# The weighted values of a key block in two pieces, the second half of the queries one slot later than the first

## The chip, the cores and the metric

One core of a Trainium2 chip runs the whole program. The metric is the time of one execution on the device in microseconds (us), lower is better. The kernel before took 1381.69 us in the median of 3 runs (1381.51 to 1382.86).

## The reference

The input x has 8 images of 256 channels and 32 x 32 pixels. Each image goes through a softmax attention over its 1024 pixels with 8 heads of 32 channels, then a linear attention and a small feed-forward net, each with a residual. The part that the change touches is the first:

```python
xn = _group_norm(xf, gn_w, gn_b)
qkv = jnp.einsum('oc,bcl->bol', w_qkv, xn) + b_qkv[None, :, None]
weight = jnp.einsum('bct,bcs->bts', q * scale, k * scale)
weight = jax.nn.softmax(weight.astype(jnp.float32), axis=1)
a = jnp.einsum('bts,bcs->bct', weight, v)
```

The softmax runs over the queries t (axis 1), so each key s has its own sum, and the values of a key can be divided by it before the last product. Behind it come the output projection and the residual, the layer norms, an elu attention with rotary angles and a short convolution ("lepe"), and a Haar transform with fc1, gelu and fc2.

## The kernel before, in words

The 8 images are pipelined. A body of the program runs the softmax attention of image i, and between its steps the later layers of image i-1 ("post" tiles: proj, x1T, lnT, qk, kT, kv, den, out, uT, ll, fc1, fc2, rT) and the norm and the projections of what comes next (gn, pq, pk, pv). A prologue stands before the first image and an epilogue behind the last. Image 0 is the body "first" (no post tiles, but small "warm" matmuls that keep TensorE busy), images 1 to 6 are "steady", image 7 is "last".

A body has 64 units: 2 groups of 4 heads, 8 blocks of 128 keys per group, 4 heads per block. For unit s, TensorE writes the scores of 128 keys and 1024 queries into one of two PSUM tiles, ps_s[s % 2], with two matmuls of 512 columns (`scores`, L636). VectorE takes the negated maximum over the queries (L1025), and ScalarE writes the exponentials to probs and their sum to sums (L887). probs holds two blocks. After the four heads of a block VectorE inverts the sums (`invert`), GpSimd (POOL) multiplies the values of the block by them (`scale`, L1297), and TensorE adds the weighted values of the block to ps_o (`weigh_values`, L651): for each half of 512 queries, 4 matmuls, one per head, each on 32 columns of the array. The profile counts each of these float32 matmuls as two records, so a block has 16. After 8 blocks ScalarE copies ps_o to att, in two halves (`copy_attention`, L896).

The order of work on each engine is written out by hand. The tables PE_FIRST, PE_STEADY, PE_LAST (L56 to L108) and their likes give, for each kind of tile, the slots in which it is issued. TensorE's loop over the slots s first issues the scores of unit s+1, then the tiles whose slot is s, in the order of the table's keys. In PE_STEADY and PE_LAST "values" is the last key, so the values come behind the other tiles of their slot. The block whose exponentials end with unit 4j+3 is weighed in a slot of the form 4j+6: 2, 6, 10, ... 62 in the steady body.

These semaphores tie the engines together around the change:

- `probs_ready`: the scores of unit s wait for the exponentials of unit s-2, which free their PSUM tile.
- `pv_done`: counts the halves of the blocks weighed. The exponentials of a block wait until both halves of the block two before it are done, since they overwrite its probs. POOL's scaling waits in the same way, and ScalarE's copy of a half waits for that half.
- `att_done`: the first block of a group may overwrite a half of ps_o only after that half was copied.
- `v_scaled_ready`: a block waits for its scaled values.

SP issues the DMAs that stack queries and keys for the scores (L450, L468), in an order of its own.

Of the kernel before, what the change touches and what calls it, by code (L numbers as in the profile page):

```python
# [16 lines left out]
NG = 2  # L17
HG, D = 4, 32
NB = L // P
# [4 lines left out]
UNITS = NG * NB * HG  # L24
# [18 lines left out]
for _name, _width in (("bq", 2), ("bk", 2), ("bproj", 2), ("bqk", 4), ("lepe_w", 6), ("lepe_bias", 6),  # L43
# [11 lines left out]

PE_FIRST = {  # L56
    "w1": (25, 28), "pq1": (11, 12), "pv1": (0, 3), "pk1": (19, 20),
    "values": (6, 10, 14, 18, 22, 26, 30, 34, 38, 42, 46, 50, 54, 58, 62), "gn": (39,), "pk0": (51, 53),
    "pq0": (44, 44), "pv0": (44, 56),
    "warm": (0, 1, 2, 3, 4, 5, 7, 8, 9, 13, 15, 16, 17, 21, 23, 24, 28, 29, 31, 32, 33, 33, 36, 37, 40, 41, 47, 48, 51, 52, 53, 57, 59, 60, 61),  # L60
}
# [19 lines left out]
    "values": (2, 6, 10, 14, 18, 22, 26, 30, 34, 38, 42, 46, 50, 54, 58, 62),  # L81
}
ACT_STEADY = {
    "copy": (3, 4, 34, 35), "x1T": (9, 10, 11, 14), "lnT": (15, 15, 16, 16),
# [20 lines left out]
    "uT": (39, 40, 43, 43), "rT": (48, 48, 50, 51), "ll": (48,), "fc1": (48, 48, 49, 49, 49, 49, 49, 49),  # L105
    "fc2": (53, 54, 56, 57), "pq1": (11, 12), "pv1": (0, 0), "pk1": (19, 19),
    "values": (2, 6, 10, 14, 18, 22, 26, 30, 34, 39, 43, 46, 50, 55, 58, 63),
}  # L108
ACT_LAST = {
    "copy": (3, 4, 36, 39), "den": (31,), "x1T": (9, 10, 11, 14), "lnT": (15, 15, 16, 16),  # L110
# [54 lines left out]
def due(engine, kind, s):  # L165

    return [(name, n) for name, slots in STEPS[engine][kind].items() for n, slot in enumerate(slots) if slot == s]
# [9 lines left out]
def tiles_of(kind):  # L177

    if kind == "prologue":
        return FIRST_TILES  # L180
    return [t for s in range(UNITS) for t in due("PE", kind, s) if t[0] not in ("values", "warm")]


def banks():


    all_banks, last = [], 1
    for kind in KINDS:
        bank, held, n = {}, None, 0
        for tile in tiles_of(kind):  # L190
            if kind == "epilogue":
                if tile not in LATER_STEPS:
                    bank[tile] = n % (2 + SPARE)
                    n += 1
            else:
                if tile == LATER_STEPS[-1]:
                    held = None
                if tile not in LATER_STEPS:
                    last = 1 - last if held is None else 1 - held
                    bank[tile] = last  # L200
                    if tile == ("fc2", 0):
                        held = last
            if tile in LATER_STEPS:
                bank[tile] = bank[("fc2", 0)]
        all_banks.append(bank)
    return all_banks


BANKS = banks()
LISTS = [[t for t in tiles_of(kind) if t not in LATER_STEPS] for kind in KINDS]  # L210


# [24 lines left out]
def build(nc, x, wqkv_t, wproj_t, wqk, fc1_t, fc2_t, params, consts, out):  # L237
    with ExitStack() as ctx:
# [88 lines left out]
        def bank(tile):  # L327
            return epilogue_banks[BANKS[writing["body"] + 1][tile]]

        def const(name):  # L330
            return con[:, CONSTS[name][0]:CONSTS[name][1]]
# [275 lines left out]
        def _(pe):  # L607
            def claim(kind, i, tile):

                before, earlier = tile_before(i, tile)  # L610
                if before is None:
                    return
                signal, per_image, after = READ[before[0]]
                b = image_of(i - earlier, before)
                here = 1 + nth_split(b, before) if before in SPLIT else after(before[1])
                pe.wait_ge(signal, per_image * b + here)
# [21 lines left out]
                                   q_st[g][:, h, half * HALF:half * HALF + HALF], start=True, stop=True)  # L638
                mm.then_inc(scores_ready, 1)

            def weigh_values(i, g, j):

                n = 2 * NB * i + NB * g + j
                pe.wait_ge(v_scaled_ready, n + 1)
                for half in range(2):
                    if j == 0 and not (isinstance(i, int) and i == 0 and g == 0):

                        pe.wait_ge(att_done, 4 * i + 2 * g - 1 + half)
                    cols = slice(half * HALF, half * HALF + HALF)
                    for h in range(HG):  # L650
                        mm = pe.matmul(ps_o[D * h:D * h + D, cols], v_scaled[:, j % 2, D * h:D * h + D],  # L651
                                       probs[:, j % 2, h, cols], start=(j == 0), stop=(j == NB - 1))
                    mm.then_inc(pv_done, 1)
# [140 lines left out]
            def step(kind, i, tile):  # L794
                name, n = tile
                if name == "warm":
                    keep_warm(kind, i, n)
                elif name == "values":
                    n = 2 * NB * i + n - (0 if kind == "first" else 1)
                    weigh_values(n // (2 * NB), n // NB % NG, n % NB)  # L800
                elif name == "w1":
                    fold(kind, i, tile)
                elif name in AHEAD:
                    pre_tile(kind, i, tile)
                else:
                    if tile not in LATER_STEPS:
                        claim(kind, i, tile)
                    post_tile(kind, i, tile)

            def fold(kind, i, tile):  # L810

                claim(kind, i, tile)
                half = tile[1]
                pe.wait_ge(late_in, LATE_LOADS)
                for c in range(NC):
                    mm = pe.matmul(bank(tile)[:, :], const("interp")[:, LL * c:LL * c + LL],
                                   fc1_nat[:, c, half * HALF:half * HALF + HALF],
                                   start=(c == 0), stop=(c == NC - 1))
                mm.then_inc(made["w1"], 1)
# [6 lines left out]
            def keep_warm(kind, i, n):  # L826

                order = [t for s in range(UNITS) for t in due("PE", kind, s)]
                later = [t for t in order[order.index(("warm", n)):] if t[0] not in ("values", "warm")]
                tile = later[0] if later else LISTS[i + 2][0]  # L830
                if later:
                    claim(kind, i, tile)
                    to = bank(tile)
                else:
                    writing["body"] = i + 1
                    claim(KINDS[i + 2], i + 1, tile)
                    to = bank(tile)
                    writing["body"] = i
                for _ in range(2):
                    pe.matmul(to[:, 0:P], const("gn_mean"), const("gn_mean"), start=True, stop=True)  # L840

            def pre_tile(kind, i, tile):
                claim(kind, i, tile)
                {"g": group_means, "q": project_heads, "k": project_heads,
                 "v": project_values}[tile[0][0 if tile[0] == "gn" else 1]](kind, i, tile)
# [12 lines left out]
            def body(kind, i, post, ahead):  # L858
                for s in range(UNITS):
                    if s + 1 < UNITS:  # L860
                        scores(i, s + 1)
                    elif ahead:
                        scores(i + 1, 0)
                    for tile in due("PE", kind, s):
                        step(kind, i, tile)

            def epilogue():
                weigh_values(B - 1, NG - 1, NB - 1)

                pe.wait_ge(probs_ready, UNITS * B)  # L870
                for s in range(UNITS):
                    for tile in due("PE", "epilogue", s):
                        step("epilogue", B, tile)
# [622 lines left out]
```

## Time and profile before

| what | value |
|---|---|
| median of 3 runs | 1381.69 us |
| the profiled execution's own time | 1382.15 us |
| its span, first to last instruction | 1380.4 us |
| granted TensorE clock, mean | 0.975 |
| busy: TensorE, VectorE, ScalarE, GpSimd | 1211.1, 991.3, 881.9, 465.6 us |
| matmuls of the scores (L636) | 1024, 404.6 us |
| matmul records of the values (L651) | 2048, 248.8 us |
| maxima (L1025) | 512, 620.0 us |
| exponentials (L887) | 512, 569.7 us |

Times of rows are in us from the start of the span. PE is TensorE's matmul stream and PEld its weight loads, DVE is VectorE, ACT ScalarE, POOL GpSimd. A busy TensorE is not TensorE at its peak, since the ends of matmuls are modelled: distances from start to start tell how fast it streams.

### The profile page before, as it was taken

How to read it: one execution, taken by the hardware profiler on the slowest of the kernel's cores; microseconds unless marked ns; L12 is line 12 of the kernel's file. 1: busy time of each engine (PE TensorE's matmuls, PEld its weight loads, DVE VectorE, ACT ScalarE, POOL GpSimd, SP SyncE). 2: the span in 40 equal slices, each digit the busy share in tenths (PEclk: the TensorE clock that was granted, in tenths of full speed). 3: DMA queues.
4: the chain of work that ended last, by engine and by line, in shares of the span. 5: the costliest groups of instructions: out<-in, count | busy, mean ns of one | idle time of the engine just before them, and what ended most of it. 6: DMA issues, size and time to landing. Idle time of an engine off the chain costs nothing.

```text
span 1380.4 us, 21964 instructions
## 1 busy us (share of the span) xinstructions
PE 1211.1 (88%) x7868; PEld 629.9 (46%) x7868; DVE 991.3 (72%) x1607; ACT 881.9 (64%) x1457; POOL 465.6 (34%) x623
## 2 busy tenths in 40 slices
PE   6888899899988999899988999899998999878846
PEld 5544544545444454444445454444444444433433
DVE  2676688848887597857889487866889487874551
ACT  1667677576766667576776768676776767656402
POOL 2001017510384015720195014730176103830450
PEclk8999999999999999999999999999999999999977
DMA  8243324133433225233252224332341333300101
GB/s 267 54 119 73 91 63 108 48 70 97 109 76 92 54 67 132 57 75 103 67 120 71 53 81 124 60 92 71 89 112 53 69 90 84 81 31 16 46 17 46
DMA packets 51355, 111.28 MB, mean 81 GB/s; under 512 B 15504, under 2 KB 15760, under 8 KB 50992
## 3 DMA queue, kind: packets, MB, share of 16 engines
q1 hardware_dynamic: 48576, 100.85, 30.0%
q0 software_dynamic: 2480, 8.78, 2.0%
q8 instruction: 63, 1.03, 0.3%
q14 instruction: 44, 0.36, 0.1%
q10 hardware_dynamic: 192, 0.26, 0.1%
HBM read 21.75 MB, written 8.39 MB: 22 GB/s over the span
## 4 chain that ended last, share of the span: by engine, by line
PE 44%; DVE 29%; POOL 8%; ACT 8%; issue 6%; SPq 3%; DMA 2%; DVEq 0%; POOLq 0%; ACTq 0%
DVE negmax L1025 15%; PE ps_s L636 10%; PE ps_o L651 7%; ACT probs L887 6%; PE work L663 4%; PE work L710 4%; POOL x L1356 4%; PE work L724 4%; PE work L782 4%; DVE ln_st L1090 3%; DVE tok L1101 3%; PE work L787 3%; POOL csum L1353 1%; DVE t L1177 1%; DVE lo L1070 1%
## 5 line engine op out<-in xcount | busy, mean ns | idle before, releaser
L887 ACT ACTIVATE probs<-ps_s,negmax 128x1024 f32<-128x1024 f32 x512 | 569.7, 1113 | 322.2 <-DVE negmax L1025 314.9
L1025 DVE TENSOR_REDUCE negmax<-ps_s 128x1 f32<-128x1024 f32 x512 | 620.0, 1215 | 192.1 <-PE ps_s L636 189.6
L636 PE MATMUL ps_s<-q_st,k_st 128*128 128x512 f32 x1024 | 404.6, 478 | 59.4 <-ACT probs L887 49.3
L636 PEld LDWEIGHTS ps_s<-q_st,k_st 128*128 128x128 f32 x1024 | 164.8, 191 | 285.5 <-ACT probs L887 167.0
L651 PE MATMUL ps_o<-probs,v_scaled 128*32 128x512 f32 x2048 | 248.8, 603 | 2.8 <-POOL v_scaled L1297 2.8
L1297 POOL TENSOR_TENSOR v_scaled<-v_tok,rsums 128x128 f32<-128x128 f32 x128 | 51.2, 400 | 545.0 <-DVE rsums L1031 544.2
L663 PE MATMUL work<-xg,w_qkv 128*128 128x512 f32 x256 | 119.6, 592 | 0.0
L724 PE MATMUL work<-ln_ch,w_qk 128*128 128x512 f32 x236 | 113.8, 604 | 2.1 <-DVE k_ch L1203 2.1
L651 PEld LDWEIGHTS ps_o<-probs,v_scaled 128*32 128x32 f32 x2048 | 53.7, 109 | 127.0 <-issue 119.8
L1356 POOL TENSOR_TENSOR x<-x,csum 128x1024 f32<-128x1024 f32 x45 | 106.8, 2373 | 2.0
L887 ACT ACTIVATION_READ_ACCUMULATOR probs<-ps_s,negmax 128x1 f32 x512 | 99.1, 194 | 0.0
L782 PE MATMUL work<-band,w 128*128 128x512 f32 x116 | 59.2, 645 | 9.1 <-ACT band L968 6.1
L663 PEld LDWEIGHTS work<-xg,w_qkv 128*128 128x128 f32 x256 | 48.2, 189 | 40.9 <-issue 33.4
L675 PEld LDWEIGHTS work<-w_qkv,xg 128*128 128x128 f32 x512 | 63.2, 196 | 4.0 <-DVE lo L1070 1.4
L675 PE MATMUL work<-w_qkv,xg 128*128 128x128 f32 x512 | 63.6, 279 | 0.0
L724 PEld LDWEIGHTS work<-ln_ch,w_qk 128*128 128x128 f32 x236 | 42.6, 190 | 41.6 <-issue 29.3
L1328 POOL TENSOR_TENSOR ln_var<-ln_mv,con 128x2 f32<-128x2 f32 x64 | 13.6, 212 | 129.0 <-DVE ln_mv L1095 129.0
L710 PE MATMUL work<-att,w_proj 128*128 128x512 f32 x120 | 56.8, 597 | 0.0
L787 PE MATMUL work<-shared,w 128*128 128x512 f32 x112 | 53.2, 597 | 1.4 <-ACT ln_ch L975 1.4
L1353 POOL TENSOR_SCALAR csum<-ln_ch,par 128x1024 f32<-128x1024 f32 x45 | 53.8, 1195 | 0.0
L971 ACT ACTIVATE shared<-work,par 128x512 f32<-128x512 f32 x58 | 39.3, 686 | 14.9 <-PE work L782 14.8
L1331 POOL TENSOR_TENSOR ln_rs<-ln_var,con 128x2 f32<-128x2 f32 x64 | 44.7, 699 | 5.0
(150 smaller groups left out, 1418.5 us busy)
## 6 DMA issues: line engine op xcount, KB each, us to landing
q_st<-hi SPq DMA_DIRECT2D x128, 128.0 KB, 2.4
q_st<-lo SPq DMA_DIRECT2D x120, 128.0 KB, 2.4
k_st<-t SPq DMA_DIRECT2D x224, 64.0 KB, 2.0
k_st<-hi SPq DMA_DIRECT2D x128, 64.0 KB, 2.0
k_st<-lo SPq DMA_DIRECT2D x128, 64.0 KB, 2.0
x<-in_x SPq DMA_DIRECT2D x8, 1024.0 KB, 4.8
out_x<-ln_ch SPq DMA_DIRECT2D x16, 512.0 KB, 2.7
xg<-in_x POOLq DMA_DIRECT2D x7, 1024.0 KB, 5.7
```

The source lines that it names most:

```text
L636: mm = pe.matmul(ps_s[s % 2][:, half * HALF:half * HALF + HALF], k_st[:, h, j * P:j * P + P], q_st[g][:, h, half * HALF:half * HALF + HALF ...
L651: mm = pe.matmul(ps_o[D * h:D * h + D, cols], v_scaled[:, j % 2, D * h:D * h + D], probs[:, j % 2, h, cols], start=(j == 0), stop=(j == NB ...
L663: mm = pe.matmul(bank(tile)[:, :], w_qkv[:, c, col:col + P], xg[:, c, half * HALF:half * HALF + HALF], start=(c == 0), stop=(c == NC - 1))
L675: mm = pe.matmul(bank(tile)[:, P * n:P * n + P], xg[:, c, P * nb:P * nb + P], w_qkv[:, c, col:col + P], start=(c == 0), stop=(c == NC - 1))
L710: mm = pe.matmul(ps[:, :], w_proj[:, g, P * c:P * c + P], att[:, g, half * HALF:half * HALF + HALF], start=(g == 0), stop=(g == 1))
L724: mm = pe.matmul(ps[:, :], w_qk[:, c, col:col + P], ln_ch[:, c, 1 + half * HALF:1 + half * HALF + HALF], start=(c == 0), stop=(c == NC - 1))
L782: pe.matmul(ps[:, :], w1[:, P * n:P * n + P], band[:, :], start=True, stop=True)\
L787: mm = pe.matmul(ps[:, :], w2[:, k, :], hid[:, k, :], start=(k == 0), stop=(k == 7))
L887: act.activation(probs[:, j % 2, h, :], ps_s[s % 2][:, :], ACT.Exp, bias=negmax[:, s % 4:s % 4 + 1], accum_out=sums[:, j % 2, h:h + 1]).th ...
L1025: dve.tensor_reduce(negmax[:, s % 4:s % 4 + 1], ps_s[s % 2][:, :], AX_X, ALU.max, negate=True)\
L1353: pool.tensor_scalar(lepe_product, ln_ch[:, c, tap:tap + L], param("lepe_w", 3 * c + tap), param("lepe_bias", 3 * c + tap), ALU.mult, ALU. ...
L1356: pool.tensor_tensor(x1[:, c, :], x1[:, c, :], lepe_product, ALU.add).then_inc(lepe_step, 1)
```

## The change

The second half of the queries of every block becomes a tile of its own, "late_values", with a table entry one slot later. The first body gets late values in slots 7, 11, ... 63, the steady body in 3, 7, ... 63, and the last body in 3, 7, ... 35, 40, 44, 47, 51, 56, 59, 63 (where the values themselves stand in 2, ... 34, 39, 43, 46, 50, 55, 58, 63, so that slot 63 has both). Behind the last image the last block is still weighed whole. In the steady and the last table the late values are the last key, behind all other tiles of their slot; in the first table they stand behind w1, pq1, pv1 and pk1 and before gn, pk0, pq0, pv0 and warm.

```diff
 PE_FIRST = {
     "w1": (25, 28), "pq1": (11, 12), "pv1": (0, 3), "pk1": (19, 20),
-    "values": (6, 10, 14, 18, 22, 26, 30, 34, 38, 42, 46, 50, 54, 58, 62), "gn": (39,), "pk0": (51, 53),
+    "values": (6, 10, 14, 18, 22, 26, 30, 34, 38, 42, 46, 50, 54, 58, 62),
+    "late_values": (7, 11, 15, 19, 23, 27, 31, 35, 39, 43, 47, 51, 55, 59, 63),
+    "gn": (39,), "pk0": (51, 53),
...
     "values": (2, 6, 10, 14, 18, 22, 26, 30, 34, 38, 42, 46, 50, 54, 58, 62),
+    "late_values": (3, 7, 11, 15, 19, 23, 27, 31, 35, 39, 43, 47, 51, 55, 59, 63),
...
     "values": (2, 6, 10, 14, 18, 22, 26, 30, 34, 39, 43, 46, 50, 55, 58, 63),
+    "late_values": (3, 7, 11, 15, 19, 23, 27, 31, 35, 40, 44, 47, 51, 56, 59, 63),
...
-            def weigh_values(i, g, j):
+            def weigh_values(i, g, j, halves=range(2)):
 
                 n = 2 * NB * i + NB * g + j
                 pe.wait_ge(v_scaled_ready, n + 1)
-                for half in range(2):
+                for half in halves:
                     if j == 0 and not (isinstance(i, int) and i == 0 and g == 0):
...
-                elif name == "values":
+                elif name in ("values", "late_values"):
                     n = 2 * NB * i + n - (0 if kind == "first" else 1)
-                    weigh_values(n // (2 * NB), n // NB % NG, n % NB)
+                    weigh_values(n // (2 * NB), n // NB % NG, n % NB, (0,) if name == "values" else (1,))
```

The lists of tiles that share the two work banks leave the late values out, as they do the values, so no tile changes its bank. The number of matmuls, their operands and the order in which the halves are added stay the same, and no DMA and no other engine's table changes.

## Rows read from the trace of the kernel before

**Rows 1.** The page: busy us (share of the span) and instructions; the chain's shares
```profile
PE 1211.1 (88%) x7868; PEld 629.9 (46%) x7868; DVE 991.3 (72%) x1607; ACT 881.9 (64%) x1457; POOL 465.6 (34%) x623
PE 44%; DVE 29%; POOL 8%; ACT 8%; issue 6%; SPq 3%; DMA 2%; DVEq 0%; POOLq 0%; ACTq 0%
```

**Rows 2.** Windows of images 0, 3 and 4: length, busy per engine, clock, DMA share, GB/s
```profile
31.00:165.00 134.00, 113.13 (x628) 64.20 (x629) 90.40 (x103) 84.56 (x141) 9.03 (x25) 0.98 0.35 87
...
483.50:643.00 159.50, 146.10 (x961) 73.92 (x960) 122.23 (x200) 110.07 (x183) 59.00 (x77) 0.99 0.34 83
643.00:801.00 158.00, 144.79 (x957) 72.81 (x956) 121.54 (x199) 109.89 (x182) 58.98 (x77) 1.00 0.34 84
```

**Rows 3.** The chain in order of time, slots 54 and 55 of image 3: start, us, what
```profile
623.54 0.47 PE ps_s L636 x2
624.01 1.85 PE ps_o L651 x16
625.86 0.66 PE ps_s L636 x2
626.52 1.72 PE work L787 x4
```

**Rows 4.** Windows inside image 3 (PE, PEld, DVE, ACT, POOL busy, clock, DMA)
```profile
507.90:516.80 8.90, 8.53 (x44) 4.02 (x42) 8.81 (x21) 6.71 (x13) 2.17 (x5) 1.00 0.14 30
521.90:531.20 9.30, 9.30 (x37) 4.14 (x37) 5.73 (x7) 6.87 (x12) 0.67 (x2) 1.00 0.37 84
574.80:597.40 22.60, 19.45 (x114) 11.27 (x110) 22.29 (x52) 14.85 (x23) 12.41 (x26) 1.00 0.28 79
616.90:629.80 12.90, 12.90 (x47) 5.98 (x46) 8.31 (x9) 7.29 (x13) 0.80 (x2) 1.00 0.11 28
```

**Rows 5.** Groups by line in image 3: busy us, mean ns, idle before, releaser
```profile
L1025 DVE TENSOR_REDUCE negmax<-ps_s 128x1 f32<-128x1024 f32 x65 | 78.7, 1214 | 21.2 <-PE ps_s L636 20.8
L887 ACT ACTIVATE probs<-ps_s,negmax 128x1024 f32<-128x1024 f32 x65 | 72.3, 1113 | 39.2 <-DVE negmax L1025 39.0
```

**Rows 6.** Timeline of TensorE, slots 9 to 11 of image 0: start, us, what
```profile
53.18 0.73 PE L636 MATMUL ps_s<-q_st,k_st 128*128 128x512 f32 x2 [1.26 <-ACT probs L887]
...
54.38 0.73 PE L636 MATMUL ps_s<-q_st,k_st 128*128 128x512 f32 x2
...
56.90 0.73 PE L636 MATMUL ps_s<-q_st,k_st 128*128 128x512 f32 x2
```

**Rows 7.** Timeline of TensorE, slots 51 to 58 of image 3
```profile
613.64 0.73 PE L636 MATMUL ps_s<-q_st,k_st 128*128 128x512 f32 x2 [0.54 <-ACT probs L887]
...
615.48 1.98 PE L787 MATMUL work<-shared,w 128*128 128x512 f32 x4 [0.24 <-ACT ln_ch L975]
616.90 1.03 PE L636 MATMUL ps_s<-q_st,k_st 128*128 128x512 f32 x2
...
625.79 0.73 PE L636 MATMUL ps_s<-q_st,k_st 128*128 128x512 f32 x2
...
631.32 0.73 PE L636 MATMUL ps_s<-q_st,k_st 128*128 128x512 f32 x2 [0.44 <-ACT probs L887]
```

**Rows 8.** Timeline of ScalarE, slots 52 to 54 of image 3
```profile
619.74 0.69 ACT L928 ACTIVATE t<-work,par 128x512 fp32r<-128x512 f32 x1 [0.59 <-PE work L663]
...
623.64 0.69 ACT L928 ACTIVATE t<-work,par 128x512 fp32r<-128x512 f32 x1 [2.11 <-PE work L663]
624.22 1.11 ACT L887 ACTIVATE probs<-ps_s,negmax 128x1024 f32<-128x1024 f32 x1
```

**Rows 9.** Timeline of TensorE, slots 32 and 39 of image 3
```profile
559.62 1.07 PE L751 MATMUL work<-shared,kmean 128*32 128x512 f32 x8 [1.06 <-POOL kmean L1371]
...
577.71 0.36 PE L681 MATMUL work<-gn_mom,con 128*128 128x4 f32 x2 [1.70 <-POOL gn_mom L1305]
```

**Rows 10.** Window at the start of the gelu stretch of image 3
```profile
600.00:603.40 3.40, 2.60 (x3) 1.17 (x4) 0.00 (x0) 3.30 (x5) 0.00 (x0) 0.59 0.91 201
```

More of the change, by code:

```diff
@@ L180, in tiles_of @@
         return FIRST_TILES
-    return [t for s in range(UNITS) for t in due("PE", kind, s) if t[0] not in ("values", "warm")]
+    return [t for s in range(UNITS) for t in due("PE", kind, s) if t[0] not in ("values", "late_values", "warm")]
 def banks():
@@ L828, in keep_warm @@
                 order = [t for s in range(UNITS) for t in due("PE", kind, s)]
-                later = [t for t in order[order.index(("warm", n)):] if t[0] not in ("values", "warm")]
+                later = [t for t in order[order.index(("warm", n)):] if t[0] not in ("values", "late_values", "warm")]
                 tile = later[0] if later else LISTS[i + 2][0]
```

## The prediction

> **What bounds the kernel now.** The reader starts with the page's busy shares: TensorE works 88% of the span and VectorE 72%, and the chain that ended last runs 44% over TensorE and 29% over VectorE [rows 1]. So TensorE comes first, but not alone. By image, the first has much idle TensorE time (113 us busy in 134) and a steady image little (146 in 159.5) [rows 2]. Some of what counts as busy is not streaming. The chain in order of time shows this around a block of values: the scores before it take 0.47 us, the block 1.85, the scores after it 0.66, and then a tile of four full matmuls 1.72 [rows 3]. A block streams four rounds of 512 columns, as such a tile does, so 1.72 is its bare work; 0.13 us is lost when TensorE goes from the full array (128*128) into the narrow form (128*32), and 0.19 us on the way back, where the weights of the next scores are not loaded ahead. One detour costs 0.32 us.
>
> The last thing to read is who is late in each stretch. Two stretches of a steady image are solid TensorE: 9.30 us of 9.30 and 12.90 of 12.90. In others VectorE is solid and TensorE is not: 8.81 against 8.53 of 8.90, and 22.29 against 19.45 of 22.60 [rows 4]. The softmax loop is the third bound. A score tile can be overwritten only after its maximum (1.21 us) and its exponential (1.11) [rows 5]; with the scores themselves (0.73 where they stand alone [rows 6]) and some 0.3 us for reading the sum and for signals, a guess, two scores of the same PSUM tile are at least about 3.35 us apart.
>
> **The change part by part.** I call slot s the stretch in which TensorE issues the scores of unit s+1 and then the tiles listed for s. All 8 matmuls of a block stood in slot 4j+2; now 4 stand there and 4 at the end of slot 4j+3, behind the tiles of that slot and behind the scores of unit 4j+4. Half a block streams 0.86 us, and with its own detour it is 0.86 + 0.32 = 1.18 us. Nothing else is added: no DMA is issued or moved, so SP's queue and POOL's are passed by nothing, and the second wait for the scaled values has been satisfied since the slot before. What leaves is 0.86 us ahead of the scores of unit 4j+4.
>
> New detours: 15 in the first image, 96 in six steady ones, 15 in the last (at slot 63 both halves stay in one slot, with no scores between). If all were exposed, the cost would be 126 x 0.32 = 40 us; if all were covered, 0. I take it stretch by stretch for a steady image.
>
> Slots 6/7 and 10/11: they feed a stretch of solid VectorE in which TensorE has 0.37 us free (8.90 less 8.53) [rows 4]. 2 x 0.32 less 0.37 gives 0.3 us. Slots 18/19: solid TensorE, 0.32 us.
>
> Slots 50/51: here the saving is wasted and the price is whole. The scores at 613.64 us waited 0.54 us for ScalarE after the block [rows 7], so they come no sooner when half of the block is gone. The late half then stands behind the transposes and the fc2 tile, which itself waits 0.24 us for ScalarE, and before the scores at 616.90. These move by 1.18 us. From there to 629.8 TensorE is solid, and ScalarE cannot make it up, since in this stretch it waits 0.59 and 2.11 us for TensorE's projection tiles [rows 8].
>
> Slots 54/55: the scores at 625.79 us follow the block directly, but the exponential on which they depend starts at 624.22 and takes 1.11 and the reading of its sum, until about 625.5 [rows 7, 8]. So only 0.26 us can be taken back here: the slip is 1.18 - 0.26 = 0.92. In slot 55 the late half follows fc2 and adds 1.18: 2.1 us. The wait of 0.44 us at 631.32 is no cover, because the exponential that ends it comes from scores issued after slot 55, which have slipped too [rows 7].
>
> The other eleven blocks I cost at nothing, and each has its cover. At 30/31 the late half stands before the scores and the denominator tile, which wait 1.06 us for kmean; the cover is nearly used up by 1.18 us. At 38/39 it stands behind the group means, which wait 1.70 us for POOL [rows 9]. The exponential of unit 40 needs the late half (probs is overwritten), so it comes later by up to 1 us. What hides it is VectorE, which from 574.8 to 597.4 us is the bound and works through a backlog of scores [rows 4]. The same backlog covers 42/43 and 46/47, and waits or backlog cover 2/3, 14/15, 22/23, 26/27, 34/35, 58/59 and 62/63. If a cover is gone, a block costs 0.32 us where TensorE never waits, and 1.18 us where a wait ahead of the late half eats the saving. ScalarE's copy of the second half at slot 35 now waits for a piece behind an output tile: about 1 us on ScalarE, ahead of an exponential whose successor on TensorE has a larger wait anyway.
>
> What is gained: in light stretches a block now pushes the scores behind it 2.52 us away from the ones before (54.38 to 56.90) [rows 6] and the pair after it closes up, so that two maxima of 1.21 us queue. With halves the scores come evenly, up to 0.37 us less per block (a pair with a block takes 56.90 - 53.18 = 3.72 us against the loop's 3.35 or so [rows 6]). For a steady image I take 0.1 us for each of four light blocks, 0.4 us; bounds 0 and 1.4.
>
> Sum of a steady image: 0.3 + 0.32 + 2.1 - 0.4 = 2.3 us, bounds -1.4 (the gain alone) and 16 x 0.32 = 5.1 from exposed detours alone; 6 images, 14 us. The last image has the early terms, one exposed detour at 55/56, less waste at 51 (nothing follows in slot 52) and some gain: 0.7 us. The first image has light blocks that gain and blocks before a projection tile (11, 19, 51) that lose up to 1 us each; I take 0, bounds -5 and +5. Together about +14.5 us.
>
> One more thing could move: the granted clock. Where TensorE stood before the gelu stretch it fell: 0.59 in a window of 3.4 us, so mostly at the lower of 1.2 and 2.4 GHz [rows 10]. The image with this fall reads 0.99 and fills 159.5 us; the next one reads 1.00 and fills 158.0 [rows 2]. TensorE's wait at slot 48 is not touched, so I take 0, with 1 us per steady image as bounds to either side, -6 and +6.
>
> The Trainium skill has two rules on the detour, and they pull apart. "TensorE: Matmul & The Clock Gate" (Part 2, step by step) says that the drain of one matmul overlaps the fill of the next and that weight loads are pulled ahead, by which a second detour would be free. "TensorEngine Tiling (Array Packing)" (Key Properties) says that changing the tiling mode drains the engine, which speaks against this change and gives no price. The 0.66 against 0.47 us sides with the second [rows 3]. By the first, the steady image would be 0 + 0 + (0.86 - 0.26 + 0.86) - 0.4 = 1.1 us and the kernel about 6 us slower; by the second the sum above stands.
>
> **Forecast.** The profiled execution took 1382.15 us, its span 1380.4, the rest lies around the program. 1382.15 + 14.5 = 1396.65; that execution is 0.46 us over the median of the runs (1381.69), so the forecast is 1396 us.
>
> **The rivals.** A, faster: the even spacing of scores decides. Its place is the first image and the light blocks of the steady ones; its price is 0.37 us for 15 + 24 blocks, 14 us, less about 4 us that the solid stretches still cost: 1372 us. For it speak VectorE's waits for scores (21 us in a steady image [rows 5]); against it, that the maxima that wait are not those that the solid stretches hold up, and that TensorE's own work in the solid stretches only grows. It decides once the late halves at 51 and 55 cost under 0.5 us together.
>
> B, no change: the gain of light blocks (1.4) and the early loss (0.6) cancel and slots 50 to 57 regain most of the 2.1 us. For it: this is one place in 16, and if ScalarE has a backlog there the slip vanishes. Against: ScalarE's waits for TensorE in just that place [rows 8]. 1382 us.
>
> C, every detour is paid and some late halves pay 1.18: 40 us for the detours, or 2.3 plus some 3 us of uncovered late halves per image: about 1382 + 32 = 1414 us. For it, TensorE is 88% busy; against, the visible waits and VectorE's solid stretches.
>
> D, slower by little: the slip at 51 is covered, only the exposed detours remain (1 us per image): 1388 us.
>
> That the change doesn't do what it says is unlikely: TensorE's order is written out by hand.
>
> **Chances.** Forecast 0.55 (its own range 1390 to 1405), C 0.10, D 0.12, A 0.14, B 0.09. A difference under 0.2%, 2.8 us, is about what a measurement of this kernel cannot tell from none. Slower: 0.55 + 0.10 + 0.12 = 0.77. Same: 0.09. Faster: 0.14. The range 1378 to 1412 holds the forecast, D, B and part of A and C.
>
> **What would show it.** Matmuls of the values in two groups of 8 records, each followed by scores of 0.66 us; the number of scores records that start behind a block doubled. The distance from the scores of unit 52 to those of 58 in a steady image about 2 us longer, and the first image unchanged within 5 us. TensorE's waits for exponentials smaller by more than the growth of its busy time would mean that rival A holds. The forecast is wrong if a steady image takes 159.5 us or less, or if scores behind a half block take 0.47 us.

## The result, and the profile after

The changed kernel takes 1425.68 us in the median of 4 runs (1423.67 to 1428.91), against 1381.92 for the kernel before beside it: a ratio of 1.0318, 95% interval 1.0294 to 1.0342, or 43.8 us more. The prediction was 1396, with a range of 1378 to 1412. The sign was right and the size was not.

The page after: busy us, chain shares, and the two groups that changed most (counts, busy, mean ns, idle before).
```profile
PE 1244.1 (87%) x7868; PEld 619.8 (43%) x7868; DVE 997.3 (70%) x1607; ACT 883.7 (62%) x1457; POOL 466.4 (33%) x623
PE 56%; DVE 22%; ACT 10%; issue 6%; POOL 2%; SPq 2%; DMA 1%; DVEq 0%; POOLq 0%; ACTq 0%
L893 ACT ACTIVATE probs<-ps_s,negmax 128x1024 f32<-128x1024 f32 x512 | 570.8, 1115 | 361.9 <-DVE negmax L1031 269.7
L657 PE MATMUL ps_o<-probs,v_scaled 128*32 128x512 f32 x2048 | 279.4, 618 | 0.8 <-POOL v_scaled L1303 0.8
```
The counts are the same. TensorE is busy 33 us longer, 31 of them in the values. The chain has moved from VectorE to TensorE (56% against 44% [rows 1]).

The waits of ScalarE, after (us in total, times, longest):
```profile
ACT probs L893 <- DVE negmax L1031: 269.7, 286, 7.9
ACT probs L893 <- PE ps_o L657: 90.2, 53, 4.1
...
ACT att L902 <- PE ps_o L657: 15.1, 14, 2.2
```
The second row has grown: exponentials wait for a late half that still reads the probs they will overwrite. Before, that was 5.6 us.

Windows after of images 0, 3, 4 and 7, set at the first exponential of each (columns as in [rows 2]):
```profile
31.80:168.00 136.20, 114.80 (x616) 60.21 (x617) 90.84 (x101) 84.53 (x141) 9.07 (x25) 0.98 0.34 84
...
498.40:663.30 164.90, 149.68 (x960) 72.33 (x959) 122.87 (x199) 110.05 (x183) 59.07 (x77) 0.99 0.33 81
663.30:829.30 166.00, 149.74 (x960) 73.10 (x959) 122.81 (x199) 110.17 (x183) 59.05 (x77) 0.99 0.33 80
1160.00:1319.80 159.80, 138.46 (x898) 64.89 (x900) 115.16 (x183) 104.45 (x175) 56.19 (x67) 0.97 0.24 57
```
Every image is longer. The first exponential of an image to that of the next takes on average 6.4 us more in the six steady images (165.3 against 159.0), 2.8 more in the first (136.2 against 133.3) and 4.9 more in the last. That is 38.2 + 2.8 + 4.9 = 45.9 us; the epilogue is 1 us shorter, and the spans of the two profiled executions are 1425.7 and 1380.4.

The chain in order of time, after, slots 54 to 56 of image 3, which answers to [rows 3]:
```profile
644.78 0.73 PE ps_s L642 x2
645.51 1.72 PE work L793 x4
647.23 1.00 PE ps_o L657 x8
648.22 0.66 PE ps_s L642 x2
648.88 1.73 PE work L793 x4
```
Half a block takes 1.00 us, of which 0.86 is streaming, and the scores behind it 0.66. So the detour is (1.00 - 0.86) + (0.66 - 0.47) = 0.33 us, where the prediction had 0.32.

### The profile page after: what moved, and what is told of

It reads as the page before. It is cut to its first block, busy times and chain, and to the rows that moved or that the text cites. A ratio compares the mean times of both kernels' runs of the same rounds, so it can differ in the third digit from the quotient of the medians.

```text
span 1425.7 us, 21979 instructions
## 1 busy us (share of the span) xinstructions
PE 1244.1 (87%) x7868; PEld 619.8 (43%) x7868; DVE 997.3 (70%) x1607; ACT 883.7 (62%) x1457; POOL 466.4 (33%) x623
## 4 chain that ended last, share of the span: by engine, by line
PE 56%; DVE 22%; ACT 10%; issue 6%; POOL 2%; SPq 2%; DMA 1%; DVEq 0%; POOLq 0%; ACTq 0%
PE ps_s L642 13%; DVE negmax L1031 10%; PE ps_o L657 10%; ACT probs L893 7%; PE work L730 6%; PE work L669 6%; PE work L716 4%; PE work L793 3%; PE work L788 3%; DVE tok L1107 2%; DVE ln_st L1096 2%; PE work L770 2%; PE work L681 2%; DVE t L1183 1%; ACT t L966 1%
## 5 line engine op out<-in xcount | busy, mean ns | idle before, releaser
L657 PE MATMUL ps_o<-probs,v_scaled 128*32 128x512 f32 x2048 | 279.4, 618 | 0.8 <-POOL v_scaled L1303 0.8
L657 PEld LDWEIGHTS ps_o<-probs,v_scaled 128*32 128x32 f32 x2048 | 41.1, 108 | 103.7 <-issue 93.4
L788 PE MATMUL work<-band,w 128*128 128x512 f32 x116 | 56.1, 616 | 10.2 <-ACT band L974 6.0
L966 ACT ACTIVATE t<-work,par_elu 128x512 f32<-128x512 f32 x59 | 40.3, 684 | 14.0 <-PE work L730 12.2
```

The lines of the kernel that those rows point to most:

```text
L788: pe.matmul(ps[:, :], w1[:, P * n:P * n + P], band[:, :], start=True, stop=True)\
L966: act.activation(elu_e[:, n % 2, :], ps[:, :], ACT.Relu, scale=-1.0, bias=par_elu[:, 0, col:col + 1]).then_inc(elu_neg_done, 1)
```

## Experiments

Three theories were set against each other. T1: late halves behind a waiting or long tile hold back exponentials and scores. T2: the detour is paid at every block. T3, formed while the first experiments ran: a split block costs 0.86 + 0.33 = 1.19 us less what the scores behind its first half really come sooner (0 to 0.86 us), and nothing where TensorE waits anyway before the next thing that counts. Differences in us are the ratio's part of 1382. From e2 on, blocks that are not named stay whole in their old slot.

**e1_late_first**: the change with late halves first in their slots.
```diff
 PE_STEADY = {
+    "late_values": (3, 7, 11, 15, 19, 23, 27, 31, 35, 39, 43, 47, 51, 55, 59, 63),
     "proj": (4, 5, 7, 8), ...
```


> All late halves stay one slot later, but stand first in their slot, directly behind the scores, instead of behind the slot's other tiles. Theory T1: about half of the 43.8 us comes from late halves that stand behind a tile that waits (group means at 39, denominator path at 31, fc2 at 51) or is long, so that the exponentials that need their probs back, and the scores behind them, come later (in the changed kernel ScalarE waits 90.2 us for ps_o, against 5.6 before). By T1 ScalarE's waits for ps_o fall under 20 us and the kernel takes 1382 + 15 to 25 = 1397 to 1407 us. Rival T2: the price is the detour through the narrow array form alone, 126 x 0.32 = 40 us, wherever the half stands: 1418 to 1428 us.

Measured: 1409.94 us, ratio 1.0197 (1.0182 to 1.0213), 27 us over before. ScalarE's waits of exponentials for ps_o fall from 90.2 to 6.2 us, but only 17 of the 44 us go. The order within the slot is a part of the loss, not half; neither T1's nor T2's time is hit. A part of these 17 us is the clock: in the profile of e1 the granted clock fell in one steady image, in that of the changed kernel in all six.

**e2_only_38** and **e8_38_late_first**: the kernel before with one block per steady image split, late half last or first in slot 39.
```diff
-    "values": (2, ..., 34, 38, 42, ...),
+    "values": (2, ..., 34, 38, 42, ...),        # of this block, the first half alone
+    "late_values": (39 for this block),         # e2: last key; e8: first key
```


> The kernel before, with the block of slot 38 alone split in the six steady images (late half behind the group means of slot 39). T1: the scores of unit 42 wait for the exponential of unit 40, which waits for the late half, which waits for POOL's moments; in the changed kernel the slip over slots 38 to 44 is 2.2 us per steady image, so 6 x 2.2 = 13 us: 1392 to 1397 us. T2: six detours, 2 us or less: 1382 to 1384 us.

> e2_only_38 with the late half first in slot 39, ahead of the transposes and of the group means that wait for POOL. T1: the exponential of unit 40 no longer waits for ps_o, and the 9 us of e2_only_38 fall to under 2: 1382 to 1385 us. T2: no change against e2_only_38, about 1391 us.

Measured: e2 1392.28, ratio 1.0062 (1.0044 to 1.0080), 8.6 us; e8 1381.59, ratio 0.9998 (0.9986 to 1.0011), nothing. T1's direction is shown: where the half stands in the slot decides. ScalarE in e2, units 39 and 40 of image 3:
```profile
578.30 1.12 ACT L893 ACTIVATE probs<-ps_s,negmax 128x1024 f32<-128x1024 f32 x1 [0.52 <-DVE negmax L1031]
...
582.19 1.11 ACT L893 ACTIVATE probs<-ps_s,negmax 128x1024 f32<-128x1024 f32 x1 [2.69 <-PE ps_o L657]
```
And TensorE in e8, slots 38 to 40 of the same image, the late half ahead of the transposes and the group means:
```profile
574.55 1.07 PE L657 MATMUL ps_o<-probs,v_scaled 128*32 128x512 f32 x8
575.55 0.66 PE L696 MATMUL work<-con,x 128*128 128x128 f32 x4
576.83 0.36 PE L687 MATMUL work<-gn_mom,con 128*128 128x4 f32 x2 [0.63 <-POOL gn_mom L1313]
577.05 0.71 PE L642 MATMUL ps_s<-q_st,k_st 128*128 128x512 f32 x2
```
In e8 the late half runs inside the time in which the group means wait for POOL (1.70 us [rows 9], now 0.63), so it costs nothing. In e2 it runs after that wait, and the exponential behind it stands 2.69 us.

The 8.6 us of e2 are not all waiting, though. Its late half, in image 3 and in image 5, and the windows around the two (clock, DMA share and GB/s last):
```profile
581.06 1.07 PE L657 MATMUL ps_o<-probs,v_scaled 128*32 128x512 f32 x8
902.31 1.82 PE L657 MATMUL ps_o<-probs,v_scaled 128*32 128x512 f32 x8
580.90:582.10 1.20, 1.20 (x11) 0.34 (x11) 1.17 (x3) 0.00 (x0) 0.67 (x1) 1.00 0.05 14
902.30:904.10 1.80, 1.80 (x10) 0.20 (x9) 1.72 (x8) 0.00 (x0) 0.52 (x1) 0.55 0.00 0
```
In image 3 the late half ran at 2.4 GHz, in image 5 mostly at 1.2 GHz. Counted from its first scores to those of unit 46, a steady image of e2 is behind the same image of before by 0.8, 0.7, 0.5, 3.9, 2.2 and 0.5 us (images 1 to 6), together 8.6. Images 4 and 5 are those in which before had no fall of the clock up to there and e2 had one while the late half ran (image 4 another one at slot 34). So an estimate from this one profile is 0.6 us per image, about 4 us, for the late half behind the wait, and about 5 us for falls of the clock. In the same stretch images 3 to 6 of e8 are within 0.2 us of before, and images 1 and 2, in which before had a fall at slot 40 and e8 had none there, are 1.2 and 1.4 us ahead. No run separates the two by itself.

**e3_only_50_54** and **e12_50_54_late_first**: the same for the two blocks of slots 50 and 54.
```diff
+    "late_values": (51, 55 for these blocks),   # e3: last key; e12: first key
```


> The kernel before, with the blocks of slots 50 and 54 alone split in the six steady images. The prediction's step gave 2.1 us per image, and the changed kernel slips by 2.07 us between the scores of units 52 and 58. T1: 6 x 2.1 = 12.5 us: 1392 to 1397 us. T2: twelve detours, 4 us: 1384 to 1387 us.

> e3_only_50_54 with the late half first in slots 51 and 55. T1 (the late half is held by tiles ahead of it, and holds exponentials): the waits of the exponentials of units 52 and 56 for ps_o (1.5 and 1.4 us) go and most of e3's 12 us with them: under 1387 us. T3 (1.19 us less what the scores behind the first half come sooner: nothing at 52, 0.3 at 56): the order within the slot changes nothing, 1.19 + 0.9 = 2.1 us per image: 1393 to 1397 us, as e3.

Measured: e3 1395.32, ratio 1.0091 (1.0074 to 1.0109), 12.6 us; e12 1395.73, ratio 1.0082 (1.0067 to 1.0098), 11.3 us. Here the order changes nothing, as T3 says and T1 does not. TensorE in e12, slots 51 to 58 of image 3, beside [rows 7]:
```profile
618.11 0.73 PE L642 MATMUL ps_s<-q_st,k_st 128*128 128x512 f32 x2 [1.40 <-ACT probs L895]
618.77 1.07 PE L657 MATMUL ps_o<-probs,v_scaled 128*32 128x512 f32 x8
...
621.10 1.98 PE L793 MATMUL work<-shared,w 128*128 128x512 f32 x4 [0.24 <-ACT ln_ch L983]
622.52 1.03 PE L642 MATMUL ps_s<-q_st,k_st 128*128 128x512 f32 x2
...
631.09 0.73 PE L642 MATMUL ps_s<-q_st,k_st 128*128 128x512 f32 x2 [0.47 <-ACT probs L895]
631.75 1.07 PE L657 MATMUL ps_o<-probs,v_scaled 128*32 128x512 f32 x8
...
637.81 0.73 PE L642 MATMUL ps_s<-q_st,k_st 128*128 128x512 f32 x2 [0.44 <-ACT probs L895]
```
The scores at 618.11 wait 1.40 us for ScalarE where they waited 0.54: the 0.86 us taken out of the block in front of them has become waiting. The same stretch that took 631.32 - 613.64 = 17.68 us before takes 637.81 - 618.11 = 19.70 us, 2.02 more. The scores at 631.09 now wait 0.47 us too, at a place where they used to follow the block directly. The changed kernel has the same (631.74 to 651.50, 19.76 us).

**e4_solid** and **e7_solid_late_first**: the same for the blocks of slots 6, 10 and 18.
```diff
+    "late_values": (7, 11, 19 for these blocks),  # e4: last key; e7: first key
```


> The kernel before, with the blocks of slots 6, 10 and 18 alone split in the six steady images, where TensorE hardly waits and no tile ahead of the late half waits. T1 and T2 agree on the detour here: 0.3 + 0.3 + 0.3 us per image less what VectorE's backlog hides, so 6 x 0.6 to 0.95 = 4 to 6 us: 1386 to 1388 us. If it is much more, something other than detours and waits is paid per split block; if nothing, the detours are hidden.

> e4_solid (blocks of slots 6, 10, 18 of the steady images split) with the late half first in its slot, ahead of the projection tile. In e4_solid the exponentials of units 8 and 20 wait 1.8 and 1.6 us for ps_o, and an image is 1.7 us longer. T1: with the late half first these waits go and what is left is the detour, 0.2 to 0.33 us per block: 6 x 0.6 to 1.0 = 4 to 6 us over before, 1386 to 1389 us. T2, which knows the detour alone, has the same time for both: e4_solid's 1394 us.

Measured: e4 1394.08, ratio 1.0075 (1.0054 to 1.0095), 10.4 us; e7 1394.39, ratio 1.0099 (1.0083 to 1.0114), 13.7 us. The order does not help, so T1 fails here too, and the waits of units 8 and 20 for ps_o cost nothing. Both are above the 4 to 6 us that T1 gave. The traces show why. Up to the scores of unit 22, three steady images of e4 are 1.0 us behind before and three 2.6 us. TensorE, slots 16 to 18 of e4, in image 3 and in image 4:
```profile
521.30 0.73 PE L642 MATMUL ps_s<-q_st,k_st 128*128 128x512 f32 x2 [0.34 <-ACT probs L893]
523.50 1.36 PE L704 MATMUL work<-con,tok 128*128 128x128 f32 x8 [1.47 <-DVE tok L1107]
...
525.51 2.89 PE L730 MATMUL work<-ln_ch,w_qk 128*128 128x512 f32 x4
...
683.00 0.73 PE L642 MATMUL ps_s<-q_st,k_st 128*128 128x512 f32 x2 [0.33 <-ACT probs L893]
685.20 1.07 PE L704 MATMUL work<-con,tok 128*128 128x128 f32 x8 [1.47 <-DVE tok L1107]
...
686.58 1.98 PE L730 MATMUL work<-ln_ch,w_qk 128*128 128x512 f32 x4
```
and the clock in windows there (the last three columns are granted clock, DMA share, GB/s):
```profile
523.50:527.00 3.50, 3.50 (x12) 2.49 (x13) 2.21 (x2) 2.73 (x6) 1.39 (x3) 0.59 0.90 203
682.50:686.00 3.50, 1.70 (x11) 1.12 (x10) 3.46 (x10) 2.67 (x7) 0.88 (x2) 1.00 0.91 204
```
The waits in front are the same 1.47 us, but in image 3 the granted clock has fallen to 1.2 GHz and a tile that takes 1.98 us takes 2.89. Without such falls e4 would cost 6 x 1.0 = 6 us; with three of them at 1.55 us this profile comes to an estimated 11 us. No steady image of the kernel before or of the changed one fell at slot 16 in its profile.

**e5_detour** and **e6_warm_behind**: nothing is moved to another slot; two small full-array matmuls stand between the halves, or behind the block.
```diff
     "values": (2, 6, 10, ...),
+    "warm": (6, 10, 18, 22),                    # e6: below late_values
+    "late_values": (2, 6, 10, ...),             # same slots as values
```


> The kernel before, but in slots 6, 10, 18 and 22 of the six steady images two small matmuls of the full array (0.11 us each, into a work bank that is free) stand between the two halves of the block. No half is moved to another slot. It is read against e6_warm_behind, where the same two matmuls stand behind the whole block. T2's detour, read from the distances of the records: the two halves with the matmuls between them take 0.32 us more than the whole block with the matmuls behind it. In time: 24 extra detours, of which those at 6, 10, 18 are not covered (0.3 us each) and that at 22 partly: 4 to 8 us over e6_warm_behind. If leaving the narrow form costs nothing, the two kernels are equal within 1 us.

> The twin of e5_detour: the same two small matmuls per block in slots 6, 10, 18 and 22 of the steady images, behind the whole block. They cost 0.22 us each time where TensorE never waits: 24 x 0.22 = 5 us at most, so 1383 to 1388 us.

Measured: e5 1406.88, ratio 1.0182 (1.0164 to 1.0201); e6 1394.78, ratio 1.0102 (1.0083 to 1.0121). The twin costs more than I gave it, since the two matmuls are four records and take 0.47 us (531.51 to 531.98 below). The difference, 11 us by the ratios, is over the 4 to 8 expected: at slot 10 the matmuls in e5 also wait for their bank (0.4 us). Slot 18 is clean. TensorE in e5 and then in e6:
```profile
536.96 1.07 PE L658 MATMUL ps_o<-probs,v_scaled 128*32 128x512 f32 x8
537.96 0.71 PE L847 MATMUL work<-con 128*128 128x128 f32 x4
538.60 1.06 PE L658 MATMUL ps_o<-probs,v_scaled 128*32 128x512 f32 x8
539.60 0.73 PE L643 MATMUL ps_s<-q_st,k_st 128*128 128x512 f32 x2
```
```profile
529.65 1.92 PE L658 MATMUL ps_o<-probs,v_scaled 128*32 128x512 f32 x16
531.51 0.71 PE L847 MATMUL work<-con 128*128 128x128 f32 x4
531.98 0.71 PE L643 MATMUL ps_s<-q_st,k_st 128*128 128x512 f32 x2
```
539.60 - 536.96 = 2.64 us against 531.98 - 529.65 = 2.33: 0.31 us for one more detour, 0.33 when the second of the two scores matmuls is taken.

**e9_waits_late_first** and **e10_other_ten**.
```diff
 e9: +    "late_values": (31, 35, 39, 43, 47 for their blocks),              # first key
 e10:+    "late_values": (3, 15, 23, 27, 31, 35, 43, 47, 59, 63 for theirs), # last key
```


> The kernel before, with the blocks of slots 30, 34, 38, 42 and 46 of the steady images split and the late half first in its slot. These are the stretches in which TensorE waits for other engines. T3 (a split block costs 1.19 us less what the scores behind its first half really come sooner, and nothing where TensorE waits anyway before the next thing that counts): no loss, and perhaps a gain, since e1_late_first makes up 0.9 us per steady image between slots 30 and 48: 1376 to 1384 us. T2 (each detour is paid): 30 x 0.33 = 10 us, 1392 us.

> The kernel before, with the ten blocks of the steady images split that e2, e3 and e4 left whole (slots 2, 14, 22, 26, 30, 34, 42, 46, 58, 62), the late half last in its slot as in the change. The changed kernel is 6.4 us per steady image slower; e2, e3 and e4 made 1.3, 2.4 and 1.7 of it. T3: these ten cost the rest, about 1 us per image, 6 us: 1385 to 1391 us. T2: 60 x 0.33 = 20 us, 1402 us.

Measured: e9 1383.29, ratio 0.9991 (0.9979 to 1.0003), no difference; e10 1389.52, ratio 1.0043 (1.0029 to 1.0056), 5.9 us. T2's 10 and 20 us are refuted; T3's figures hold. e9's possible gain does not show. The clock helped e10: in its profile one steady image had a fall, in that of before five. Its five images without one take 156.7 to 157.7 us from their first scores to their last, against 156.0 in the one image of before without one, so at an equal clock the ten blocks would cost nearer 8 us than 6 (an estimate).

**e11_first_last**: the change in the bodies "first" and "last" alone.
```diff
 PE_STEADY = {
-    "late_values": (3, 7, ..., 63),
+    (none; every block whole)
```


> The change in the first and the last image alone; the six steady images are as before. In the trace of the changed kernel the first image is 2.8 us and the last 4.9 us longer. If the parts add up (T3), 7.7 us: 1390 to 1393 us. The prediction had 0 and 0.7 us here: 1383 us. T2: 29 or 30 detours at 0.33, 10 us: 1393 us, so T2 is told apart from T3 by the trace of the first image alone (2.8 against 5 us).

Measured: 1389.69, ratio 1.0042 (1.0029 to 1.0055), 5.8 us; the first image is 2.4 us longer and the last 4.3 in its trace. The last image alone is a weak witness: in e9 and e10, where it was not changed, it took 156.1 and 156.8 us from its first exponential to its last, against 154.9 before.

## Why the prediction was wrong, point by point

What each experiment measured, beside what the prediction's steps gave for the same blocks:

| blocks split | predicted, us | measured, us |
|---|---|---|
| steady 50, 54 | 6 x 2.1 = 12.6 | 12.6 |
| steady 6, 10, 18 | 6 x 0.62 = 3.7 | 10.4 |
| steady 38 | 0 | 8.6 |
| steady, the other ten | 0, gain of 6 x 0.4 = -2.4 | 5.9 |
| first and last image | 0.7 | 5.8 |
| sum | 14.6 | 43.3 |
| the whole change | 14.5 | 43.8 |

The parts add up, but in part by luck, because each measured part holds its own falls of the clock. The three falls at slot 16 in e4, some 4.7 of its 10.4 us, occur in no steady image of the changed kernel, and e10 was spared falls that before had. Image 4, the only steady image in which before had no fall, shows the changed kernel's loss itself: it is behind by 1.4 us at the scores of unit 22, 2.9 at unit 38, 5.2 at unit 46 (with one fall, at slot 40), 5.3 at unit 52, 7.35 at unit 59 and 7.7 at unit 63.

**Right: the detour** (0.32 predicted, 0.33 measured), and that it is paid on top of the streaming. **Right: slots 50 to 57.** The saving is wasted at 51, the price there is whole, about 0.3 us is taken back at 55 (0.26 predicted). The changed kernel's scores of units 52 to 59 slip by 2.08 us against 2.1.

**Wrong: "What hides it is VectorE, which ... works through a backlog of scores" (38/39).** The prediction saw that the exponential of unit 40 would come later, and that the late half stood behind the wait of 1.70 us. It then took VectorE's solid stretch as cover. But the backlog is one score deep: there are two score tiles, and the scores of unit 42 wait for the exponential of unit 40. In the changed kernel, ScalarE and then TensorE (image 3):
```profile
596.41 1.11 ACT L893 ACTIVATE probs<-ps_s,negmax 128x1024 f32<-128x1024 f32 x1 [3.41 <-PE ps_o L657]
```
```profile
594.26 0.36 PE L687 MATMUL work<-gn_mom,con 128*128 128x4 f32 x2 [1.76 <-POOL gn_mom L1311]
594.55 1.81 PE L657 MATMUL ps_o<-probs,v_scaled 128*32 128x512 f32 x8
596.29 1.22 PE L642 MATMUL ps_s<-q_st,k_st 128*128 128x512 f32 x2
```
e8 shows that the order is the cause: the block costs nothing once the late half stands ahead of that wait. In the images without a new fall of the clock there it costs about 0.6 us; the rest of e2's 8.6 us goes with the clock at 1.2 GHz behind the wait, as in the rows above, where the late half takes 1.81 us. The prediction had set the clock's part at nothing, with TensorE's wait at slot 48 in view; the falls that the change brought stand behind the wait of slot 39.

**Wrong in size: slots 6, 10 and 18.** The terms of 0.3 and 0.32 us counted detours alone and took the saving of 0.86 us as always realized. At unit 8 the scores could come only 0.7 us sooner, because the exponential of unit 6 ended then; so 0.5 us is left of 1.19, not 0.33. Together 1.0 us per image instead of 0.62, and falls of the clock for the rest of e4.

**Wrong: the covers of the other ten, and the gain of even spacing.** Scores behind a first half do come up to 0.86 us sooner, but those behind the late half come later by the detour or more, and no stretch keeps the gain: the ten cost 1 us per image where 0.4 was to be gained. The rule by which I worked out 50/54 (1.19 less what the next scores gain) was at hand, and I did not apply it to them.

**Wrong: first and last image.** Blocks before a projection tile lose as solid ones do (in the first image the scores of unit 53 come 1.2 us later behind those of unit 52 than before), and the gains I set against them did not come.

Of the rivals, A, B and D are refuted by the time; C named 1414 us and the right kind of loss (late halves that find no cover), but its sum by detours alone is refuted by e9 and e10. "No cover is lost" and "every cover is lost" were both wrong; what tells them apart is where the half stands against the nearest wait, which C did not say.

What stays open: the parts were each measured in runs that spread by up to 8 us, so the agreement of 43.3 with 43.8 could not be better than a few us even with equal clocks. Of the 43.8 us, how much is the clock and how much the order of work is not shown. The ten blocks were not taken apart further, nor were the 5.8 us of the first and last image. No version beat the kernel before; e8 and e9 equal it.

## What to carry to other kernels

A piece of work that is split and pushed one step back does not only cost its overhead: it can cost its whole length again where the step it was taken from ends in a wait for another engine, for the time taken out becomes waiting there (slots 50 and 51). Where the step it moves into still has a wait behind the piece, it costs nothing (e9). Before moving a piece, ask for each place which wait ends next in front of it and behind it. If other engines need the piece, it belongs ahead of the wait (e8 against e2); in a solid stretch its place in the slot made no difference (e12 against e3, e7 against e4). And a backlog covers a delay only as deep as the buffers that hold it.

## What was not expected of the hardware

The granted clock falls at places that small shifts of the schedule choose. In the changed kernel it fell at slot 39 or 40 in all six steady images, behind the wait for the group means (window of image 3 after, and the stretch before it):
```profile
591.30:594.60 3.30, 1.51 (x12) 1.15 (x16) 3.22 (x12) 1.21 (x2) 0.79 (x4) 1.00 0.01 2
594.70:598.10 3.40, 3.40 (x14) 1.62 (x8) 2.15 (x8) 1.21 (x2) 1.69 (x6) 0.50 0.02 5
```
TensorE was busy 1.51 of 3.30 us at 2.4 GHz, and then had 1.2 GHz just while the late half ran, which took 1.81 us instead of 1.06. In the kernel before, five of the six steady images had a fall, at slots 37 to 48, with late halves first (e1) only one had, and in e2 there were eight. In e4 a fall costs 1.55 us, so how many occur moves this kernel by several us, and it may be a part of the spread of its runs. Each count is from one profiled execution, and this was not tested by itself.
